# A fused two-expert feed-forward layer: direct block products in the first step, the second layer's tiles in one row, splits in two groups, another mix at the end

## The chip, the cores and the metric

The kernel runs on one core of a Trainium2 chip. The metric is device time in microseconds for one execution, from runs on the chip. Before the change the median of three runs is 2035.06 us (2034.77 to 2036.32).

## What is computed

For each of 8 batches, with x of 512 tokens by 512 features, a shared feed-forward network and one of five experts, chosen by the batch's label, are applied to the same x, and mixed by a gate that looks at token 0 only:

```python
ffn(x, wi0, wi1, wo) = (gelu(x @ wi0) * (x @ wi1)) @ wo          # 512 -> 2048 -> 512
share_out  = ffn(x, sWi0, sWi1, sWo)
expert_out = ffn(x, Wi0[label], Wi1[label], Wo[label])
gate_in = concatenate([expert_out[:, 0], share_out[:, 0]])
w = softmax(relu(gate_in @ g0) @ g1)
out = x + expert_out * w[0] + share_out * w[1]
```

All arrays are float32.

## The kernel before, in words

**Steps.** There are 128 steps: 8 batches, in each the shared network and then the expert, in each of those 8 steps of 256 hidden units. A step works on a 2 by 2 block scheme (two halves of the hidden units, two halves of the features, two halves of the tokens). Seven block products P1 to P7 of sums of blocks take the place of eight; the sums of weight blocks are made by VectorE (`weight_sums`, L493 to L515: one of 512 elements per partition, one of 1024 that makes two sums, one of 512), those of x by GpSimd once for each batch (`moving_sums`, L670).

**Splits.** TensorE multiplies in the type fp32r. Each operand is split in a high part, which ScalarE casts (`a_hi` L356, `x_hi` L366, `wo_hi`, `hid_hi` L391), and a low part, which VectorE makes by a subtraction (`lo`, L491). Each product of the reference is then three matmuls (low by high, high by low, high by high). The seven weight operands are split in groups of 3, 3 and 1, always for the step after the present one (`ahead(g)`). The high and low weights (`a_op`) have one buffer, the loaded weights (`a_src`) two, the split hidden units (`hs`) two.

**TensorE's order** is written out by hand (`step`, L281). A block product (`product`, L263) is 12 matmuls of 256 columns; one tile of the second layer (`second`, `down` L273) is 6 matmuls of 512 columns into `ps_out`. A step is P1, P5, tile 3, P6, P2, tile 0, P7, P3, tile 1, P4, tile 2. Tiles 0 to 2 use the hidden units of the step before, tile 3 those of two steps before. All engines execute their queue in the order of the program and wait on semaphores.

**ScalarE** copies partial products between PSUM banks (`p1_copied`, `v_copied`, `u_copied`, L426 to L449) and into `p5`, takes the three Gelus of a step (L398), and makes the high parts. After step 3 of a shared pass it takes the exponential of the gate (`exponentials`, L461).

**VectorE** (`step`, L533) makes, in this order: the weight sums for the next step, the low part of Wo, the low parts ahead, the product for block 11 (L554), the additions for blocks 22 and 12 (L558, L560), the product of 512 elements (L562), that for block 21 (L565), the remaining low parts ahead, and last the low part of this step's hidden units. Between two steps stands the gate's work (`one_pass`, L621): `gate_half` (L572, four dot products) after expert step 3; `gate_half` and the logits after shared step 1; `shift_logits` after shared step 2; `gate_weights` and `combine_shared` (2048 elements per partition) after shared step 3; `combine_expert` (L618) after shared step 4. The last six belong to the batch before, so the first batch's shared pass has none.

**SyncE** issues every DMA in its program order: Wo for the next step once the raw buffer is free, then the weights for the step after that, group by group.

**The start and the end.** In the first step the seven products are split one by one in the order P1, P5, P6, P2, P7, P3, P4. After the last step, the gate of the last batch is computed with nothing beside it. ScalarE and VectorE then scale tiles of the shared output, GpSimd adds x to two of them (L707), and VectorE adds the expert's tiles (L661), each of which is stored as it is ready.

Of the kernel before, what the change touches and what calls it, by code (L numbers as in the profile page):

```python
# [5 lines left out]
F32 = mybir.dt.float32  # L6
# [7 lines left out]
P = 128  # L14
# [17 lines left out]
ORDER = (P1, P5, P6, P2, P7, P3, P4)  # L32


GROUPS = [(0, 3), (3, 6), (6, 7)]
LAST_OF = (P6, P3, P4)
# [5 lines left out]
def splits(m, g):  # L42

    if m == 0:
        return GROUPS[g][1]
    return m * 3 + (PRODUCTS - 3 + g + 1)


def build(nc, x_cols, x_rows, labels, experts, shared, g0_rows, g1_rows, out):
# [10 lines left out]
    with ExitStack() as ctx:  # L60
# [14 lines left out]
        hs = [[sb(f"hid{s}{p}", [P, 2, TOK], F32R) for p in "hl"] for s in range(2)]  # L75
# [28 lines left out]
        ps_p5 = bank("ps_p5")  # L104
        ps_c11 = bank("ps_c11")
        ps_v = bank("ps_v")
# [3 lines left out]
        def halves(ps):  # L110
            return ps[:, :].rearrange("p (a t) -> p a t", a=2)
# [18 lines left out]
        wo_ready = sem("wo_ready")  # L130
        p_done = [sem(f"p_done{i}") for i in range(PRODUCTS)]
# [23 lines left out]
        last_scaled = sem("last_scaled")  # L155
        last_based_pool = sem("last_based_pool")
        last_based_dve = sem("last_based_dve")
        last_mixed = sem("last_mixed")

        block = ctx.enter_context(nc.Block())  # L160

# [13 lines left out]
        def _(sp):  # L175
# [23 lines left out]
            def first_loads():  # L199
                load_a(SHARED, None, 0, 0, 0, 0, first_a[P1])  # L200
                load_b(x_cols[0], 0, 0, first_b[P1])
                load_a(SHARED, None, 0, 0, 1, 0, first_a[P7])
                load_a(SHARED, None, 0, 0, 1, 1, first_a[P4])
                load_b(x_cols[0], 0, 1, first_b[P7])
                load_b(x_cols[0], 1, 1, first_b[P3])
                load_a(SHARED, None, 0, 0, 0, 1, first_a[P2])
                load_b(x_cols[0], 1, 0, first_b[P2])
                for i, j in A_PLACE:
                    load_a(SHARED, None, 1, 1, i, j, w_loaded[1])
                load_wo(SHARED, None, 0)  # L210
                sp.dma_start(labels_sb[:, :], labels).then_inc(labels_loaded, 16)

            def next_x(b):

                sp.wait_ge(x_ready, splits(b, 2))
                cols = x_cols[bass.ds(b + 1, 1)].rearrange("b p k t -> (b p) k t")
                for j, k in B_PLACE:
                    load_b(cols, j, k, x_loaded)

            def one_pass(b, net, n0, first, last):  # L220
# [5 lines left out]
                for c in range(STEPS):  # L226

                    ahead = c + 1
# [3 lines left out]

                    ahead = c + 2
                    if not (last and ahead >= STEPS):
                        of = net if ahead < STEPS else 1 - net
                        sp.wait_ge(a_ready, splits(n0 + c, 0))
                        load_a(of, label, ahead % STEPS, c % 2, 0, 0, w_loaded[c % 2])
                        sp.wait_ge(a_ready, splits(n0 + c, 1))
                        load_a(of, label, ahead % STEPS, c % 2, 0, 1, w_loaded[c % 2])
                        load_a(of, label, ahead % STEPS, c % 2, 1, 0, w_loaded[c % 2])  # L240
                        sp.wait_ge(a_ready, splits(n0 + c, 2))
                        load_a(of, label, ahead % STEPS, c % 2, 1, 1, w_loaded[c % 2])
# [19 lines left out]
        def _(pe):  # L262
            def product(i, ps, fresh):  # L263
                for a in (GATE, LIN):
                    for k in range(2):
                        for h, (ap, xp) in enumerate(PASSES):
                            mm = nc.tensor.matmul(ps[:, a * HALF:(a + 1) * HALF], a_op[ap][:, i, a, k, :],  # L267
                                                  x_op[xp][:, i, k, :],
                                                  start=(fresh and a == 0 and k == 0 and h == 0),
                                                  stop=(a == 1 and k == 1 and h == 2), skip_group_check=True)  # L270
                mm.then_inc(p_done[i], 1)

            def down(m, s, start, stop):  # L273
                for f in range(2):
                    for h, (hp, wp) in enumerate(PASSES):
                        mm = nc.tensor.matmul(ps_out[m][:, :], hs[s][hp][:, f, m * P:(m + 1) * P], wo[s][wp][:, f, :],  # L276
# [3 lines left out]

            def step(n, c, b, net, first, last):  # L281


                s = c % 2
                very_first = first and c == 0
                new_x = net == SHARED and c == 0

                def operands(i):
                    if very_first:
                        pe.wait_ge(a_ready, ORDER.index(i) + 1)  # L290
                        pe.wait_ge(x_ready, ORDER.index(i) + 1)
                    elif i in (P1, P2, P4):
                        g = (P1, P2, P4).index(i)
                        pe.wait_ge(a_ready, splits(n, g))
                        if new_x:
                            pe.wait_ge(x_ready, splits(b, g))

                def second(m):
                    before = 2 if m == MC - 1 else 1
                    if first and c < before:  # L300
                        return
                    of = (c - before) % STEPS
                    if m == 0:
                        pe.wait_ge(hid_ready, n)
                        pe.wait_ge(wo_ready, n)
# [5 lines left out]
                operands(P1)  # L311
                if not very_first:

                    pe.wait_ge(product_done, n * 3 - 2)
                product(P1, ps_c11, True)
                operands(P5)
                if not very_first:
                    pe.wait_ge(c12_done, n)
                product(P5, ps_p5, True)
                second(3)  # L320
                operands(P6)
                pe.wait_ge(p1_copied, n + 1)
                product(P6, ps_v, False)
                operands(P2)
                product(P2, ps_c11, False)
                second(0)
                operands(P7)
                pe.wait_ge(v_copied, n + 1)
                product(P7, ps_v, False)
                operands(P3)  # L330
                product(P3, ps_p5, False)
                second(1)
                operands(P4)
                pe.wait_ge(u_copied, n + 1)
                product(P4, ps_c21, False)
                second(2)

            def one_pass(b, net, n0, first, last):
                for c in range(STEPS):
                    step(n0 + c, c, b, net, first, last)  # L340

            pe.wait_ge(idle_ready, 1)

            for i in range(IDLE_MATMULS):
                nc.tensor.matmul((ps_v if i % 2 else ps_c21)[:, :], idle[:, 0:P], idle[:, :], start=True, stop=True)
            schedule(one_pass)

            down(3, 0, False, False)
            pe.wait_ge(hid_ready, N_STEPS)
            pe.wait_ge(wo_ready, N_STEPS)  # L350
            for m in range(MC):
                down(m, 1, False, True).then_inc(last_down_done, 1)

        @block.scalar
        def _(sc):
            def a_hi(m, s, g):  # L356


                sc.wait_ge(p_done[LAST_OF[g]], m)

                sc.wait_ge(sums_done, m * 3 + (2 if g == 0 else 3))
# [3 lines left out]
            def x_hi(b, g, n):  # L365

                sc.wait_ge(p_done[LAST_OF[g]], n + 1)
                sc.wait_ge(x_sums_done, b * 4 + (3 if g < 2 else 4))
# [3 lines left out]
            def first_hi(i):  # L372
                if i in (P5, P6, P7, P3):
                    sc.wait_ge(sums_done, {P5: 1, P6: 2, P7: 2, P3: 3}[i])
                else:
                    sc.wait_ge(first_a[i], 16)
                nc.scalar.copy(a_op[HI][:, i, :, :, :], a_src[0][:, i, :, :, :]).then_inc(a_hi_done, 1)
                if i in (P5, P6, P7, P4):
                    sc.wait_ge(x_sums_done, {P5: 1, P7: 2, P6: 3, P4: 4}[i])
                else:  # L380
# [3 lines left out]
            def wo_hi(n, s, free):  # L384
                sc.wait_ge(wo_loaded, n * 32 + 32)
                if free:
# [4 lines left out]
            def hid_hi(n, s, free):  # L391
                sc.wait_ge(product_done, n * 3 + 3)
                if free:
                    sc.wait_ge(down_done, n * MC - MC)
                nc.scalar.copy(hs[s][HI][:, :, :], act[:, LIN, :, :]).then_inc(hid_hi_done, 1)
# [3 lines left out]

            def step(n, c, b, net, first, last):  # L400
                s = c % 2
                very_first = first and c == 0
# [3 lines left out]
                free = not first or c > 1  # L406
# [3 lines left out]

                def ahead(g):
                    if not very_last:
                        a_hi(n + 1, 1 - s, g)
                    if new_x:
                        x_hi(b + 1, g, n)
# [5 lines left out]
                sc.wait_ge(p_done[P1], n + 1)  # L421
                if not very_first:

                    sc.wait_ge(c22_done, n)
                    sc.wait_ge(c12_done, n)
                nc.scalar.copy(ps_v[:, :], ps_c11[:, :]).then_inc(p1_copied, 1)  # L426
                if not first and c == 1:
                    copy_out(2)
                sc.wait_ge(p_done[P5], n + 1)
                nc.scalar.copy(p5[:, :, :], halves(ps_p5)).then_inc(p5_saved, 1)  # L430
                wo_hi(n, s, free)
                if not first and c == 1:
                    copy_out(3)
                sc.wait_ge(p_done[P6], n + 1)
                sc.wait_ge(p5_saved, n + 1)
                nc.scalar.copy(ps_p5[:, :], ps_v[:, :]).then_inc(v_copied, 1)
# [315 lines left out]
```

## Time and profile before

| | before |
|---|---|
| median of 3 runs | 2035.06 us |
| the profiled execution's own time | 2034.56 us |
| its span, first to last instruction | 2032.8 us |
| granted TensorE clock, mean | 0.995 |
| TensorE matmul busy | 2006.0 us (99%) |
| VectorE busy | 1631.2 us (80%) |
| ScalarE busy | 1221.1 us (60%) |
| GpSimd busy | 87.7 us (4%) |

Matmuls are pipelined and overlap, so busy time alone does not say how fast TensorE runs; the distance between the starts of two neighbours does. In the rows, PE is TensorE's matmul part, PEld its weight loads, DVE VectorE, ACT ScalarE, POOL GpSimd, SP SyncE. L12 is line 12 of the kernel. Times are microseconds unless marked ns, and start times count from the start of the span.

### The profile page before, as it was taken

The numbers are of one execution on the slowest core, as the hardware profiler recorded it, in microseconds if no ns is written. First come the engines' busy times: TensorE is split into PE (matmuls) and PEld (weight loads), VectorE is DVE, ScalarE is ACT, GpSimd is POOL, SyncE is SP. The second block draws the span as 40 slices with busy tenths as digits, with TensorE's granted clock in tenths as the row PEclk, the third lists the DMA queues.
The fourth block names the chain that finished last, engine by engine and source line by source line (L and its number), as shares of the span: only waits on it lengthen the run. The fifth ranks groups of instructions, "written<-read, shape, count | busy, mean of one in ns | idle before, by whom it ended". The sixth has DMA issues, their size and how long they took to land.

```text
span 2032.8 us, 34874 instructions
## 1 busy us (share of the span) xinstructions
PE 2006.0 (99%) x13834; PEld 1869.4 (92%) x13834; DVE 1631.2 (80%) x1917; ACT 1221.1 (60%) x1665; POOL 87.7 (4%) x62
## 2 busy tenths in 40 slices
PE   7999999999999999999999999999999999999997
PEld 6999999999999999999999999999999999999996
DVE  8778888787887878878788787887878878788785
ACT  6555566655666566655665656666566665665653
POOL 1001000010000100001000010000100010000000
PEclk8999999999999999999999999999999999999998
DMA  5333333433334332243333433344333433324330
GB/s 197 105 114 115 94 94 122 138 115 115 96 102 135 120 120 94 95 155 124 96 94 118 157 99 94 113 131 130 99 98 116 135 115 118 101 94 147 114 94 31
DMA packets 188020, 230.87 MB, mean 114 GB/s; under 512 B 13266, under 2 KB 152530, under 8 KB 185810
## 3 DMA queue, kind: packets, MB, share of 16 engines
q1 hardware_dynamic: 187858, 228.65, 35.3%
q8 instruction: 109, 1.79, 0.4%
q14 instruction: 53, 0.43, 0.1%
HBM read 220.21 MB, written 8.39 MB: 112 GB/s over the span
## 4 chain that ended last, share of the span: by engine, by line
PE 97%; DVE 1%; DMA 0%; ACT 0%; POOLq 0%; issue 0%; SPq 0%; POOL 0%; ACTq 0%
PE ps_out L276 35%; PE ps_c L267 27%; PE ps_p L267 18%; PE ps_v L267 18%; DVE al L491 0%; DMA a_src<-shared 0%; POOLq L60 0%; DVE xl L491 0%; DVE gate_prod L581 0%; ACT ah L363 0%; DVE a_src L515 0%; SPq L191 0%; SPq L182 0%; DVE hid1l L491 0%; DVE a_src L511 0%
## 5 line engine op out<-in xcount | busy, mean ns | idle before, releaser
L491 DVE TENSOR_TENSOR al<-a_src,ah 128x1536 fp32r<-128x1536 f32 (+1 forms) x388 | 532.6, 1398 | 63.0 <-ACT ah L363 60.1
L363 ACT CAST ah<-a_src 128x1536 fp32r<-128x1536 f32 x381 | 451.8, 1186 | 69.4 <-DVE a_src L511 69.4
L267 PE MATMUL ps_c<-xh,al 128*128 128x256 f32 x1536 | 433.6, 282 | 1.5 <-DVE xl L491 0.8
L267 PE MATMUL ps_c<-xh,ah 128*128 128x256 f32 x1536 | 434.6, 283 | 0.0
L267 PE MATMUL ps_c<-xl,ah 128*128 128x256 f32 x1536 | 434.6, 283 | 0.0
L267 PEld LDWEIGHTS ps_c<-xh,al 128*128 128x128 f32 x1536 | 293.9, 191 | 13.3 <-issue 1.4
L267 PEld LDWEIGHTS ps_c<-xl,ah 128*128 128x128 f32 x1536 | 293.9, 191 | 9.8
L267 PE MATMUL ps_p<-xh,al 128*128 128x256 f32 x1024 | 290.5, 284 | 6.4 <-DVE xl L491 6.4
L267 PEld LDWEIGHTS ps_c<-xh,ah 128*128 128x128 f32 x1536 | 293.9, 191 | 0.0
L267 PE MATMUL ps_v<-xh,al 128*128 128x256 f32 x1024 | 289.2, 282 | 2.9 <-ACT ps_v L426 2.9
L267 PE MATMUL ps_p<-xl,ah 128*128 128x256 f32 x1024 | 290.3, 284 | 0.0
L267 PE MATMUL ps_p<-xh,ah 128*128 128x256 f32 x1024 | 290.3, 284 | 0.0
L267 PE MATMUL ps_v<-xh,ah 128*128 128x256 f32 x1024 | 290.3, 284 | 0.0
L267 PE MATMUL ps_v<-xl,ah 128*128 128x256 f32 x1024 | 290.2, 283 | 0.0
L398 ACT ACTIVATE act<-act 128x512 f32<-128x512 f32 x128 | 80.9, 632 | 244.4 <-DVE act L560 244.4
L267 PEld LDWEIGHTS ps_v<-xh,al 128*128 128x128 f32 x1024 | 196.0, 191 | 14.5 <-DVE al L491 2.1
L267 PEld LDWEIGHTS ps_v<-xl,ah 128*128 128x128 f32 x1024 | 196.1, 191 | 9.8
L276 PE MATMUL ps_out<-wo1h,hid1l 128*128 128x512 f32 x512 | 203.3, 397 | 0.5 <-DVE hid1l L491 0.5
L267 PEld LDWEIGHTS ps_p<-xh,al 128*128 128x128 f32 x1024 | 197.1, 192 | 6.6 <-issue 6.6
L276 PE MATMUL ps_out<-wo0h,hid0l 128*128 128x512 f32 x512 | 202.5, 395 | 0.0
L276 PE MATMUL ps_out<-wo0l,hid0h 128*128 128x512 f32 x512 | 202.3, 395 | 0.0
L276 PE MATMUL ps_out<-wo1l,hid1h 128*128 128x512 f32 x512 | 202.3, 395 | 0.0
(75 smaller groups left out, 3598.9 us busy)
## 6 DMA issues: line engine op xcount, KB each, us to landing
a_src<-shared SPq DMA_DIRECT2D x256, 256.0 KB, 4.3
a_src<-experts SPq DMA_DIRECT2D x256, 256.0 KB, 4.2
raw_wo<-shared SPq DMA_DIRECT2D x128, 256.0 KB, 2.9
raw_wo<-experts SPq DMA_DIRECT2D x128, 256.0 KB, 2.8
x_src<-x_cols SPq DMA_DIRECT2D x32, 256.0 KB, 5.8
x_res<-x_rows SPq DMA_DIRECT2D x8, 1024.0 KB, 10.1
out<-s_out SPq DMA_DIRECT2D x7, 1024.0 KB, 8.4
g_sb<-g_rows SPq DMA_DIRECT2D x1, 2048.0 KB, 9.6
```

The lines of the kernel that those rows point to most:

```text
L267: mm = nc.tensor.matmul(ps[:, a * HALF:(a + 1) * HALF], a_op[ap][:, i, a, k, :], x_op[xp][:, i, k, :], start=(fresh and a == 0 and k == 0 ...
L276: mm = nc.tensor.matmul(ps_out[m][:, :], hs[s][hp][:, f, m * P:(m + 1) * P], wo[s][wp][:, f, :], start=(start and f == 0 and h == 0), stop ...
L363: nc.scalar.copy(a_op[HI][:, i:j, :, :, :], a_src[s][:, i:j, :, :, :]).then_inc(a_hi_done, 1)
L398: nc.scalar.activation(to, of, ACT.Gelu_apprx_tanh).then_inc(gelu_done, 1)
L491: nc.vector.tensor_tensor(to, of, hi.bitcast(F32), ALU.subtract).then_inc(done, 1)
```

## The change

**First step.** Step 0 takes eight products of the blocks as they are loaded, with no sums. VectorE makes the sums of x for the first batch. **Row of four.** In steps 1 to 127 the four tiles of the second layer stand in one row, after P2, all from the hidden units of the step before; in the very last step two stand there and two after P4. The split hidden units have one buffer. **Two groups.** The weight operands are split in groups of 4 and 3; the second group of a step's own weights is split in that step. The Gelu and the product of block 21, and the split of the hidden units, move to the head of the next step in ScalarE's and VectorE's queues. SyncE issues the weights before Wo. **End.** The last split of hidden units is in two parts, VectorE alone adds x and the scaled shared output, and GpSimd's and ScalarE's part in this goes.

The diff, cut to its core:

```diff
-GROUPS = [(0, 3), (3, 6), (6, 7)]
-LAST_OF = (P6, P3, P4)
+GROUPS = [(0, 4), (4, 7)]
+LAST_OF = (P2, P4)
...
-        hs = [[sb(f"hid{s}{p}", [P, 2, TOK], F32R) for p in "hl"] for s in range(2)]
+        hs = [sb(f"hid{p}", [P, 2, TOK], F32R) for p in "hl"]
...
@@ tensor @@
+            def first_step():
+                pe.wait_ge(a_ready, 1)
+                pe.wait_ge(x_ready, 1)
+                product(P1, P1, ps_c11, True)
+                pe.wait_ge(a_ready, 2)
+                pe.wait_ge(x_ready, 2)
+                product(P2, P2, ps_c11, False).then_inc(direct_done, 1)
...
+                product(P7, P7, ps_v, True)
+                product(P4, P3, ps_v, False).then_inc(direct_done, 1)
...
+                pe.wait_ge(a_ready, a_splits(n, 0))
...
+                pe.wait_ge(product_done, n * 3 - 2)
+                product(P1, P1, ps_c11, True).then_inc(p_done[P1], 1)
...
+                product(P5, P5, ps_p5, True).then_inc(p_done[P5], 1)
+                moving(P6)
+                pe.wait_ge(p1_copied, n)
+                product(P6, P6, ps_v, False).then_inc(p_done[P6], 1)
+                product(P2, P2, ps_c11, False).then_inc(p_done[P2], 1)
+                pe.wait_ge(hid_ready, n)
+                pe.wait_ge(wo_ready, n)
+                very_last = last and c == STEPS - 1
+                for m in range(2 if very_last else MC):
+                    second(m)
+                pe.wait_ge(a_ready, a_splits(n, 1))
...
+                product(P7, P7, ps_v, False).then_inc(p_done[P7], 1)
+                product(P3, P3, ps_p5, False).then_inc(p_done[P3], 1)
...
+                product(P4, P4, ps_c21, False).then_inc(p_done[P4], 1)
...
@@ scalar, step @@
+                c21_gelu()
+                sc.wait_ge(p_done[P1], n)
...
+                nc.scalar.copy(ps_v, ps_c11[:, :]).then_inc(p1_copied, 1)
+                hid_hi(n - 1, 0, TOK)
...
+                nc.scalar.copy(p5[:, :, :], halves(ps_p5)).then_inc(p5_saved, 1)
+                a_hi(n, s, 1)
...
+                nc.scalar.copy(ps_p5, ps_v).then_inc(v_copied, 1)
+                if not very_last:
+                    a_hi(n + 1, 1 - s, 0)
...
@@ scalar, end @@
-                nc.scalar.activation(s_out[:, m, :], s_out[:, m, :], ACT.Copy, scale=gate_w[:, SHARED:SHARED + 1]
-                                     ).then_inc(last_scaled, 1)
...
@@ vector, step @@
+                c21_product(n - 1)
+                if not very_last:
+                    weight_sums(n + 1, 1 - s, 0)
+                    weight_sums(n + 1, 1 - s, 1)
+                hid_lo(n - 1, 0, TOK)
...
+                    weight_sums(n + 1, 1 - s, 2)
+                a_lo(n, s, 1)
...
+                    a_lo(n + 1, 1 - s, 0)
...
+                dve.wait_ge(hid_ready, n)
+                c11_product(n)
+                wo_lo(n, s)
...
@@ vector, end @@
+            combine_shared(BATCH - 1)
+            dve.wait_ge(mixed, BATCH * 2 - 1)
             for m in range(MC):
-                if m < MC // 2:
-                    dve.wait_ge(last_based_dve, m + 1)
-                else:
-                    dve.wait_ge(last_based_pool, m + 1 - MC // 2)
                 dve.wait_ge(last_down_done, m + 1)
...
@@ gpsimd, end @@
-            pool.wait_ge(x_res_loaded, BATCH * 16)
-            for m in range(MC // 2, MC):
-                pool.wait_ge(last_scaled, m + 1 - MC // 2)
-                nc.gpsimd.tensor_tensor(s_out[:, m, :], x_res[:, m, :], s_out[:, m, :], ALU.add
-                                        ).then_inc(last_based_pool, 1)
```

The additions for blocks 22 and 12 and the product of 512 elements still end VectorE's step, and the gate's work still stands between two steps, at the same places.

## Rows read from the trace of the kernel before

**Rows 1.** The page's busy time of each engine, share of the span, instructions.
```profile
PE 2006.0 (99%) x13834; PEld 1869.4 (92%) x13834; DVE 1631.2 (80%) x1917; ACT 1221.1 (60%) x1665; POOL 87.7 (4%) x62
```
**Rows 2.** The chain that ended last, in order of time: start, length, what.
```profile
38.58 1.44 PE ps_p L267 x12
40.02 1.39 PE ps_out L276 x6
...
44.23 1.43 PE ps_c L267 x12
```
**Rows 3.** Timeline around the last step's end: start, length, engine, line, operation, tiles.
```profile
2006.69 0.69 DVE L560 TENSOR_TENSOR act<-ps_p,p 128x512 f32<-128x512 f32 x1
...
2007.47 0.63 ACT L398 ACTIVATE act<-act 128x512 f32<-128x512 f32 x1 [1.66 <-DVE act L560]
...
2008.14 0.69 DVE L562 TENSOR_TENSOR act<-act 128x512 f32<-128x512 f32 x1 [0.76 <-ACT act L398]
...
2009.19 0.28 PE L267 MATMUL ps_c<-xh,ah 128*128 128x256 f32 x1
...
2009.51 0.38 ACT L398 ACTIVATE act<-ps_c 128x256 f32<-128x256 f32 x1 [1.40 <-PE ps_c L267]
...
2009.93 0.42 DVE L565 TENSOR_TENSOR act<-act,ps_c 128x256 f32<-128x256 f32 x1 [1.09 <-ACT act L398]
...
2010.38 1.05 ACT L395 CAST hid1h<-act 128x1024 fp32r<-128x1024 f32 x1 [0.49 <-DVE act L565]
...
2011.47 1.23 DVE L491 TENSOR_TENSOR hid1l<-act,hid1h 128x1024 fp32r<-128x1024 f32 x1 [1.12 <-ACT hid1h L395]
...
2012.74 0.50 PE L276 MATMUL ps_out<-wo1h,hid1l 128*128 128x512 f32 x1 [0.53 <-DVE hid1l L491]
...
2014.24 0.39 PE L276 MATMUL ps_out<-wo1h,hid1l 128*128 128x512 f32 x1
...
2015.60 0.39 PE L276 MATMUL ps_out<-wo1h,hid1l 128*128 128x512 f32 x1
```
**Rows 4.** Timeline of VectorE where the gate's work stands between two steps.
```profile
203.04 0.68 DVE L581 CUSTOM_DVE_ANT_0 gate_prod<-g_sb,gate_row 128x512 f32<-128x512 f32 x1
...
205.85 0.69 DVE L506 TENSOR_TENSOR a_src<-a_src 128x512 f32<-128x512 f32 x1
...
296.79 0.75 DVE L581 CUSTOM_DVE_ANT_0 gate_prod<-g_sb,gate_row,gate_sum 128x512 f32<-128x512 f32 x1
...
300.34 0.69 DVE L506 TENSOR_TENSOR a_src<-a_src 128x512 f32<-128x512 f32 x1
301.07 1.23 DVE L511 TENSOR_TENSOR a_src<-a_src 128x1024 f32<-128x1024 f32 x1
...
327.99 0.16 DVE L603 RECIPROCAL gate_inv<-gate_den 128x1 f32<-128x1 f32 x1
...
330.71 0.69 DVE L506 TENSOR_TENSOR a_src<-a_src 128x512 f32<-128x512 f32 x1
```
**Rows 5.** Groups by line on VectorE: the expert's mixing, one each batch but the last.
```profile
L618 DVE SCALAR_TENSOR_TENSOR s_out<-x_src,gate_w,s_out 128x2048 f32<-128x2048 f32 x7 | 16.4, 2346 | 0.0
```
**Rows 6.** Timeline of ScalarE around one exponential of the gate.
```profile
325.76 1.28 ACT L463 ACT_TABLE_LOAD   x1
...
334.25 1.28 ACT L398 ACT_TABLE_LOAD   x1
```
**Rows 7.** Timeline of VectorE where GpSimd's sums of x begin.
```profile
171.84 1.78 DVE L506 TENSOR_TENSOR a_src<-a_src 128x512 f32<-128x512 f32 x1
```
**Rows 8.** Busy time of one early stretch by engine; third from last the granted clock.
```profile
14.30:20.00 5.70, 3.86 (x16) 3.60 (x17) 5.70 (x9) 5.70 (x11) 0.96 (x1) 0.50 0.00 0
```
**Rows 9.** Timeline of VectorE in the first step.
```profile
9.97 0.81 DVE L515 TENSOR_TENSOR a_src<-a_src 128x512 f32<-128x512 f32 x1 [0.85 <-DMA a_src<-shared]
```
**Rows 10.** Timeline of VectorE at the end.
```profile
2021.08 0.23 DVE L605 TENSOR_SCALAR gate_w<-gate_exp,gate_inv 128x2 f32<-128x2 f32 x1
...
2029.39 0.75 DVE L661 SCALAR_TENSOR_TENSOR s_out<-ps_out,gate_w,s_out 128x512 f32<-128x512 f32 x1 [0.47 <-POOL s_out L708]
```

More of the change, by code:

```diff
@@ L226, in one_pass @@
                 for c in range(STEPS):
+                    ahead = c + 2
+                    if not (last and ahead >= STEPS):
+                        of = net if ahead < STEPS else 1 - net
+                        sp.wait_ge(a_ready, a_splits(n0 + c, 0))
+                        load_a(of, label, ahead % STEPS, c % 2, 0, 0, w_loaded[c % 2])
+                        load_a(of, label, ahead % STEPS, c % 2, 0, 1, w_loaded[c % 2])
+                        sp.wait_ge(a_ready, a_splits(n0 + c, 1))
+                        load_a(of, label, ahead % STEPS, c % 2, 1, 0, w_loaded[c % 2])
+                        load_a(of, label, ahead % STEPS, c % 2, 1, 1, w_loaded[c % 2])
                     ahead = c + 1
@@ L262, in _, with product @@
         def _(pe):
-            def product(i, ps, fresh):
+            def product(i, j, ps, start):
                 for a in (GATE, LIN):
@@ L279, in down, with moving @@
                 return mm
-            def step(n, c, b, net, first, last):
[L284 to L296, printed above, removed]
-                def second(m):
[L299 to L305, printed above, removed]
+            def first_step():
[5 more added lines that the diff above has]
+                product(P2, P2, ps_c11, False).then_inc(direct_done, 1)
+                pe.wait_ge(x_ready, 3)
+                product(P1, P7, ps_p5, True)
+                pe.wait_ge(x_ready, 4)
+                product(P2, P3, ps_p5, False).then_inc(direct_done, 1)
+                pe.wait_ge(a_ready, 3)
+                product(P7, P1, ps_c21, True)
+                pe.wait_ge(a_ready, 4)
+                product(P4, P2, ps_c21, False).then_inc(direct_done, 1)
+                product(P7, P7, ps_v, True)
+                product(P4, P3, ps_v, False).then_inc(direct_done, 1)
+            def step(n, c, b, net, first, last):
+                def moving(i):
+                    if n == 1 and i in (P5, P6, P7, P4):
+                        pe.wait_ge(x_ready, {P5: 5, P6: 6, P4: 7, P7: 8}[i])
+                    if n > 1 and net == SHARED and c == 0 and i in (P1, P7):
+                        pe.wait_ge(x_ready, x_splits(b, 0 if i == P1 else 1))
+                def second(m):
+                    of = (c - 1) % STEPS
                     if of == 0 and not first:
@@ L323, in step @@
[L323 to L336, printed above, removed]
+                pe.wait_ge(a_ready, a_splits(n, 0))
@@ L338, in one_pass @@
+                moving(P4)
+                pe.wait_ge(u_copied, n)
+                product(P4, P4, ps_c21, False).then_inc(p_done[P4], 1)
+                if very_last:
+                    for m in range(2, MC):
+                        second(m)
             def one_pass(b, net, n0, first, last):
-                for c in range(STEPS):
+                for c in range(1 if first else 0, STEPS):
                     step(n0 + c, c, b, net, first, last)
@@ L397, in gelu, with c21_gelu, first_step @@
             def gelu(to, of):
                 nc.scalar.activation(to, of, ACT.Gelu_apprx_tanh).then_inc(gelu_done, 1)
+            def c21_gelu():
+                gelu(act[:, GATE, 1, 0:HALF], ps_c21[:, 0:HALF])
+            def first_step():
+                for i in (P1, P2):
+                    first_a_hi(i)
+                    first_x_hi(i)
+                for i in (P7, P3):
+                    first_x_hi(i)
+                for i in (P7, P4):
+                    first_a_hi(i)
+                a_hi(1, 1, 0)
+                for i, done in ((P5, 1), (P6, 2), (P4, 3)):
+                    sc.wait_ge(x_sums_done, done)
+                    first_x_hi(i)
+                gelu(act[:, GATE, 0, 0:HALF], ps_c11[:, 0:HALF])
+                wo_hi(0, 0)
+                sc.wait_ge(direct_done, 4)
+                sc.wait_ge(x_sums_done, 4)
+                nc.scalar.copy(x_op[HI][:, P7, :, :], x_src[:, P7, :, :]).then_inc(x_hi_done, 1)
+                gelu(act[:, GATE, :, HALF:TOK], ps_pv[:, :, 0:HALF])
@@ L431, in step @@
[L431 to L436, printed above, removed]
-                ahead(0)
-                sc.wait_ge(p_done[P2], n + 1)
+                if n > 1:
+                    sc.wait_ge(p_done[P4], n - 1)
+                c21_gelu()
+                sc.wait_ge(p_done[P1], n)
@@ L444, in step @@
-                    copy_out(0)
-                sc.wait_ge(p_done[P7], n + 1)
-                if not very_first:
-                    sc.wait_ge(product_done, n * 3)
-                nc.scalar.copy(ps_c21[:, :], ps_v[:, :]).then_inc(u_copied, 1)
-                sc.wait_ge(c22_done, n + 1)
-                sc.wait_ge(c12_done, n + 1)
-                gelu(act[:, GATE, :, HALF:TOK], act[:, GATE, :, HALF:TOK])
-                ahead(1)
-                if not first and c == 0:
-                    copy_out(1)
@@ L456, in step @@
-                sc.wait_ge(p_done[P4], n + 1)
-                gelu(act[:, GATE, 1, 0:HALF], ps_c21[:, 0:HALF])
-                ahead(2)
-                hid_hi(n, s, free)
+                        sc.wait_ge(x_ready, x_splits(b, 0))
+                    for m in range(MC):
+                        copy_out(m)
+                sc.wait_ge(p_done[P7], n)
+                sc.wait_ge(product_done, n * 3)
+                nc.scalar.copy(ps_c21[:, :], ps_v).then_inc(u_copied, 1)
+                sc.wait_ge(c22_done, n)
@@ L466, in one_pass @@
             def one_pass(b, net, n0, first, last):
-                for c in range(STEPS):
+                for c in range(1 if first else 0, STEPS):
                     step(n0 + c, c, b, net, first, last)
@@ new lines, in step @@
+            def step(n, c, b, net, first, last):
+                s = c % 2
+                very_last = last and c == STEPS - 1
+                c21_product(n - 1)
[3 more added lines that the diff above has]
+                hid_lo(n - 1, 0, TOK)
+                if n == 1:
+                    first_x_lo(P7, 8)
+                if not very_last:
+                    weight_sums(n + 1, 1 - s, 2)
+                a_lo(n, s, 1)
+                if n > 1 and net == SHARED and c == 0:
+                    x_lo(b, 1)
+                if not very_last:
+                    a_lo(n + 1, 1 - s, 0)
+                if net == EXPERT and not last and c == STEPS - 1:
+                    x_lo(b + 1, 0)
+                dve.wait_ge(hid_ready, n)
+                c11_product(n)
+                wo_lo(n, s)
+                dve.wait_ge(u_copied, n)
+                dve.wait_ge(p5_saved, n)
@@ L621, in one_pass @@
             def one_pass(b, net, n0, first, last):
-                for c in range(STEPS):
-                    step(n0 + c, c, b, net, first, last, (n0 + c + 2) // 2)
+                for c in range(1 if first else 0, STEPS):
+                    step(n0 + c, c, b, net, first, last)
                     if net == EXPERT and c == 3:
```

277 lines of the change are left out of this document (128 added, 149 removed).

## The prediction

> **What bounds the kernel now.** I read the page's busy time first: TensorE is busy for 2006.0 of 2032.8 us, no other engine for more than 80% [rows 1]. Busy matmuls overlap, so I then read the chain that ended last, in order of time. From about 44 us to 2009 us it consists of TensorE's own pieces, one directly behind the other: a product takes 1.44 us, a tile of the second layer 1.39 us [rows 2]. Seven products and four tiles make 7 × 1.44 + 4 × 1.39 = 15.64 us, a step's period to the rounding (15.61 without it). So in the middle only two things count: TensorE's own pace, and whether a wait of TensorE that is free today stops being free. The start and the end stand beside that.
>
> **The pace of the row of four.** Each six-matmul tile of the steady part takes 1.39 us, always behind a product [rows 2]. After the last step four tiles stand in a row: the second starts at 2014.24, the third at 2015.60, so a tile behind a tile takes 1.36 us [rows 3]. The row of four gains 3 × 0.03 = 0.09 us a step. A part is lost: a product behind a tile takes 1.43, one behind a product 1.44 [rows 2], and three such neighbours fewer cost 0.03. Net 0.06 us in each of 126 steps: **−7.6 us**. The Trainium skill (TensorE: Matmul & The Clock Gate, section "Wait — 56ns, not 53.3ns?") gives a warm matmul's start-to-start as N ÷ 2.4 GHz plus about 2.5 ns, whatever stands beside it, 216 ns for 512 columns. By that rule the order gains nothing and this term is zero. The rows show 232 and 227 ns per matmul (1.39 and 1.36 by six), and depend on the neighbour, so I take the rows.
>
> **Whether the waits stay free, ordinary step.** I lay the new queues beside TensorE's, T = 0 at the first matmul of P1. P2 ends and the row of four begins at T = 4 × 1.44 = 5.76; with 1.39 + 3 × 1.36 it ends at 11.23, P4 at 15.54. The row waits for the low part of the hidden units of the step before. Its chain, from the latencies in rows 3:
> - P3's last matmul is at −1.56. A reader starts 0.32 behind the last matmul (2009.19 to 2009.51), so the addition for block 12 is at −1.24. Its Gelu is 0.78 later (2006.69 to 2007.47), −0.46; the product of 512 elements 0.67 later, +0.21. VectorE is free again at about 0.81.
> - Block 21's Gelu is at +0.20, its product on VectorE at 0.81, because VectorE is busy. Behind it stand the first sum (1.15) and the double sum (1.88, since 0.73 passes between those two starts [rows 4]), then at 3.02 the hidden units' low part. ScalarE copies P1's partial result at 1.64, then makes the high part at about 2.15; the low part follows 1.09 later [rows 3], at 3.24. TensorE can go on 1.27 later (2011.47 to 2012.74), at 4.51.
>
> That leaves 1.25 us of slack. P6 waits for ScalarE's copy, done at 2.2, needed at 2.88: free. The step's second weight group (1536 elements; about 1.5 us high, 1.7 low) is ready near 7, needed at 11.23: free. The first group ahead is ready near 10.2, needed at 15.54: free. One split operation fewer (7 operands in two groups instead of three) saves VectorE under 0.1 us, hidden. SyncE's new order brings weights before Wo; Wo's split is now only at about 8, so both are covered by several microseconds, at zero; so is the single buffer of hidden units, whose readers end at 11.23 before the new split at about 17.7. The new PSUM layout costs nothing.
>
> **Where they do not stay free.** The gate's work stands between two steps on VectorE. Before, the hidden units were already split when it began; now block 21's product and the hidden units' low part queue behind it. With extra work X at 0.81 the low part starts at 3.02 + X, TensorE can go on at 4.29 + X, and waits X − 1.47 at the row of four, with nothing else that it may do.
> - Half of the gate after expert step 3: X = 205.85 − 203.04 = 2.81 [rows 4], a wait of 1.34, 8 times: 10.7 us.
> - Half of the gate and the logits after shared step 1: X = 300.34 − 296.79 = 3.55 [rows 4], 2.08, 7 times: 14.6 us.
> - Gate weights and shared mixing after shared step 3: 330.71 − 327.99 = 2.72 of work [rows 4]. It needs the exponential first. ScalarE is free at 0.1, loads a table (1.28), and has the exponential at about 1.7; before, this fell in time that nobody needed. Work from 1.74 to 4.46 makes X = 3.65, a wait of 2.18, 7 times: 15.3 us. A second table load of 1.28 us before the next Gelu exists today too [rows 6]; it now comes before the copy that P6 needs, so some 0.9 of the 2.18 shows at P6.
> - Expert mixing after shared step 4: 2.35 us [rows 5], 2.26 to the next start, 0.79, 7 times: 5.5 us.
> - Each row or product behind a wait starts slower: the tile from 2012.74 takes 1.50 instead of 1.39 [rows 3]; 36 waits by 0.1: 3.6 us.
>
> Together **+49.7 us**. The shift of the logits (0.3 us) fits in the slack. Part of the slack is taken in 7 steps by GpSimd's sums of x, beside which VectorE's 0.69 us operation took 1.78 [rows 7]: up to 1.1 each; it should be just covered, 0 taken, +7.7 as the upper end.
>
> **The start.** Before, P1 of step 2 starts at 44.1 [rows 2]; at the half clock (1.2 GHz) TensorE spent 14.3 to 20 us [rows 8], after some 6 us with nothing to do. Now loads land in the order they are used: the seventh landed by 9.97 before [rows 9], the same place holds the seventh now. Splits of 0.6 to 0.7 us each let the eight products run from 6.2 to 18.7 with gaps under 1 us. Step 1's sums, splits of four operands, sums of x on VectorE and a Gelu table load put its P1 at about 24.6 and its row at 31.3 at full clock, so step 2 at 41.1: a gain of 3.0. But TensorE stands idle for 6 us before P1, as it did when the clock fell, and I charge 1.6 for a few microseconds at half: **−1.4 us**, between −3 and +1.
>
> **The end.** Before, P4's end lies at 2009.31 and the last four tiles start at 2012.74. Now after P4 come two tiles (2.75), then, because of the single buffer, high and low parts of a quarter: 0.25 until readable, 0.42, 0.42 and 0.04 make 3.88 until the last four can start, instead of 3.43. But before P4 this step holds two tiles (2.75) instead of three (4.17). 0.45 − 1.42 makes −0.97, of which the neighbours of the pace paragraph give back some: **−0.9 us**. The gate's chain is unchanged up to its weights (done at 2021.3 [rows 10]). Before, GpSimd's part held the last mixing until 2029.39; now VectorE mixes 2048 elements (2.35 [rows 5]) and starts the fourth tile at 2021.34 + 2.39 + 3 × 0.67 = 2025.74: 3.65 earlier; some 0.15 comes back as four stores lie closer: **−3.5 us**.
>
> **Sum.** −7.6 + 49.7 − 1.4 − 0.9 − 3.5 = **+36.3 us**. The profiled execution took 2034.56 (the median is 0.5 above, no difference here), so 2070.9 us; the last digit of the latencies is worth 0.3 to 1 us over 29 places, and I say **2070 us**.
>
> **Rivals.**
> - *The hidden units are in time (faster).* Place: the row's wait after the gate's work. Were the slack over 2.2 us larger than I worked out (it decides at X − 1.47 > 0 for the largest X of 3.65), the 49.7 go and −13.4 is left: 2021 us. For it: in the trace before, TensorE waits for nothing in these steps. Against: there the split stood ahead of the gate's work. 0.09. Part of it, a slack some 0.5 to 1 us larger (12 to 25 us less): 2045 to 2058: 0.12.
> - *No gain in pace.* If the 1.36 of the end, where other engines rest, is not reached in mid-step, the lost 0.03 stays: +3.8 in place of −7.6, 2082 us. 0.08.
> - *The clock falls at the waits.* A gap of 0.5 us at 2012.3 left it at full; one of 6 us ended at half [rows 8]. The new gaps lie between. Were it half for 8 us after each of the 22 places with over 1.3 us (8 + 7 + 7), 22 × 4 = 88 more: 2158 us. 0.05.
> - *Nothing to measure:* slack larger by 0.8 us and the exponential free; 2031 to 2039. 0.04.
> - The forecast: 0.62, between 2056 (slack 0.5 larger) and 2083 (GpSimd's 7.7 and no pace gain).
>
> A measurement here can tell 0.2%, 4 us. Faster holds the first rival, 0.09; same 0.04; slower all else, 0.87. The range 2050 to 2084 leaves out the first of these, the clock, no change, and a little of the part case.
>
> **What would show it.** In the profile after: the chain with VectorE's hidden-unit low part (line of `lo`) in 29 places and ScalarE's copy in 7; tiles 2 to 4 of a row at 1.36; an ordinary period of 15.54; four waits per batch at the row, about 1.3, 2.1, 2.2 (with P6's part) and 0.8 us; no GpSimd piece at the end. Wrong: TensorE's waits for hidden units sum to under 25 us, or stretches of half clock after 50 us.

## The result and the profile after

| | before | after |
|---|---|---|
| median of the runs | 2035.05 us (4) | 2073.1 us (4: 2070.88 to 2073.45) |
| ratio, 95% interval | | 1.0183 (1.0166 to 1.0201) |
| profiled execution | 2034.56 us | 2070.88 us |
| its span | 2032.8 us | 2069.1 us |

The change costs 38 us by the medians, 36.3 us by the two profiled executions, on which the sum below is made. The profiled execution is the shortest of its four, 2.2 us under their median; so where an experiment below is set against the changed kernel, the medians show some 2 us more than the profiles. The forecast was 2070, between 2050 and 2084. The page of the kernel after, busy time and the chain that ended last by engine:

```profile
PE 2008.9 (97%) x13846; PEld 1874.3 (91%) x13846; DVE 1612.3 (78%) x1780; ACT 1180.3 (57%) x1524; POOL 88.0 (4%) x56
...
PE 86%; DVE 11%; ACT 2%; issue 1%; DMA 0%; SPq 0%; POOL 0%; DVEq 0%; ACTq 0%; POOLq 0%
```

Beside [rows 1] VectorE and ScalarE are less busy than before (GpSimd is as before, 88.0 beside 87.7 us), and yet VectorE now holds 11% of the chain. An engine can do less and come later. The view of waits, TensorE's alone (line, whom it waited for, us in total, times, longest):

```profile
PE ps_out L276 <- DVE hidl L519: 34.4, 30, 1.9
PE ps_pv L267 <- ACT ps_pv L459: 6.9, 7, 1.0
PE ps_c L267 <- DVE act L574: 5.1, 1, 5.1
```

The first line is the second layer's first tile, 29 times in mid-run and once at the end; the second is P6 behind ScalarE's copy, 7 times; the third is the start. The view counts from a matmul's modelled end; by the distances between starts, which are used from here on, each wait is some 0.15 us longer. One of the thirty, in the timeline (VectorE's rows and TensorE's):

```profile
200.34 0.69 DVE L651 CUSTOM_DVE_ANT_0 gate_prod<-g_sb,gate_row 128x512 f32<-128x512 f32 x1
200.96 0.08 DVE L651 DVE_READ_ACCUMULATOR2_ANT gate_sum<- 128x1 f32 x1
200.96 0.41 DVE L579 TENSOR_TENSOR act<-act,ps_c 128x256 f32<-128x256 f32 x1
201.29 0.68 DVE L532 TENSOR_TENSOR a_src<-a_src 128x512 f32<-128x512 f32 x1
202.01 1.23 DVE L536 TENSOR_TENSOR a_src<-a_src 128x1024 f32<-128x1024 f32 x1
...
202.97 0.28 PE L267 MATMUL ps_c<-xh,ah 128*128 128x256 f32 x1
203.16 1.22 DVE L519 TENSOR_TENSOR hidl<-act,hidh 128x1024 fp32r<-128x1024 f32 x1
...
204.43 0.50 PE L276 MATMUL ps_out<-wo1h,hidl 128*128 128x512 f32 x1 [1.18 <-DVE hidl L519]
```

The last dot product of the gate, then block 21's product, two sums, the hidden units' low part, and 1.27 us after its start TensorE's tile: the queue of the prediction, piece by piece. P2's last matmul starts at 202.97; without the wait the tile would start 0.12 later, so 1.34 us are lost.

And the pace, in the chain in order of time, an ordinary step after [rows 2 show one before]:

```profile
46.41 1.44 PE ps_c L267 x12
47.85 5.47 PE ps_out L276 x24
53.32 2.87 PE ps_pv L267 x24
```

Four tiles take 5.47 us, not 4 × 1.39 = 5.56, and the two products behind them 2.87. The start-to-start distances of all matmuls give the whole account:

| part | before | after | difference |
|---|---|---|---|
| start of the span to P5 of step 2 | 45.50 | 43.37 | −2.13 |
| P5 of step 2 to P5 of step 127 | 1951.03 | 1993.88 | +42.85 |
| from there to TensorE's last matmul | 21.57 | 20.71 | −0.86 |
| from there to the end of the span | 14.69 | 11.15 | −3.54 |
| sum | 2032.8 | 2069.1 | +36.3 |

The second line holds 45.9 us of waits (below), 29 + 7 slow restarts of 0.11 and 0.10 (3.9 us) and one stretch at half clock (about 1.6, below), together 51.4. From this the pace goes off, 125 × 0.06 = 7.5 us (the ordinary period is 15.54 us, before 15.60), and 1.0 us more, because in the kernel before seven steps, the first of each new batch, were 0.15 longer than the others, and now are not.

### The profile page after: what moved, and what is told of

Read it like the earlier page. It is cut to its first block, busy times and chain, and to the rows that moved or that the text cites. A ratio compares the mean times of both kernels' runs of the same rounds, so it can differ in the third digit from the quotient of the medians.

```text
span 2069.1 us, 34457 instructions
## 1 busy us (share of the span) xinstructions
PE 2008.9 (97%) x13846; PEld 1874.3 (91%) x13846; DVE 1612.3 (78%) x1780; ACT 1180.3 (57%) x1524; POOL 88.0 (4%) x56
## 4 chain that ended last, share of the span: by engine, by line
PE 86%; DVE 11%; ACT 2%; issue 1%; DMA 0%; SPq 0%; POOL 0%; DVEq 0%; ACTq 0%; POOLq 0%
PE ps_out L276 34%; PE ps_pv L267 31%; PE ps_c L267 21%; DVE gate_prod L651 2%; DVE a_src L536 2%; DVE hidl L519 2%; DVE act L637 1%; ACT act L411 1%; DVE s_out L683 1%; DVE a_src L532 1%; DVE s_out L688 1%; DVE act L579 0%; ACT L492 0%; DMA a_src<-shared 0%; DVE act L639 0%
## 5 line engine op out<-in xcount | busy, mean ns | idle before, releaser
L519 DVE TENSOR_TENSOR al<-a_src,ah 128x1536 fp32r<-128x1536 f32 (+2 forms) x258 | 524.8, 2035 | 103.0 <-ACT ah L377 94.4
L267 PE MATMUL ps_pv<-xh,al 128*128 128x256 f32 x2048 | 580.0, 283 | 6.9 <-ACT ps_pv L459 6.9
L267 PE MATMUL ps_pv<-xl,ah 128*128 128x256 f32 x2048 | 579.9, 283 | 0.0
L267 PE MATMUL ps_pv<-xh,ah 128*128 128x256 f32 x2048 | 579.9, 283 | 0.0
L377 ACT CAST ah<-a_src 128x2048 fp32r<-128x2048 f32 x254 | 430.7, 1696 | 43.2 <-PE ps_c L267 38.8
L267 PEld LDWEIGHTS ps_pv<-xh,al 128*128 128x128 f32 x2048 | 393.1, 192 | 13.3 <-ACT ps_pv L459 8.3
L267 PEld LDWEIGHTS ps_pv<-xl,ah 128*128 128x128 f32 x2048 | 393.0, 192 | 5.0
L267 PEld LDWEIGHTS ps_pv<-xh,ah 128*128 128x128 f32 x2048 | 393.0, 192 | 0.0
L276 PE MATMUL ps_out<-wo1h,hidl 128*128 128x512 f32 x512 | 203.1, 397 | 30.0 <-DVE hidl L519 30.0
L276 PE MATMUL ps_out<-wo0h,hidl 128*128 128x512 f32 x512 | 200.8, 392 | 4.4 <-DVE hidl L519 4.4
```

What stands on the lines that cost most here:

```text
L276: mm = nc.tensor.matmul(ps_out[m][:, :], hs[hp][:, f, m * P:(m + 1) * P], wo[s][wp][:, f, :], start=(start and f == 0 and h == 0), stop=(s ...
L377: nc.scalar.copy(a_op[HI][:, i:j, :, :, :], a_src[s][:, i:j, :, :, :]).then_inc(a_hi_done, 1)
L519: nc.vector.tensor_tensor(to, of, hi.bitcast(F32), ALU.subtract).then_inc(done, 1)
```

## The experiments

All times are medians beside runs of the kernel before on the same chip (2034.9 to 2035.3 us).

**1. The gate's work behind the hidden units.**

```diff
+            def gate_between(b, net, first, c):
+                if net == EXPERT and c == 4:
+                    gate_half(b, 0, SHARED)
...
                 hid_lo(n - 1, 0, TOK)
+                gate_between(b, net, first, c)
...
                     step(n0 + c, c, b, net, first, last)
-                    if net == EXPERT and c == 3:
-                        gate_half(b, 0, SHARED)
```

> The changed kernel, with one edit: on VectorE the gate's work that stood between two steps stands one place later, behind the low part of the hidden units in the next step; ScalarE's exponential stays where it is. Theory (queue order): the row of four waits only because block 21's product and the hidden units' low part queue behind the gate's work. The waits at the row, 8 x 1.34, 7 x 2.08, 7 x 1.03 and 7 x 0.79 us in the profile after, go with their slow restarts (29 x 0.11), together 36 to 42 us; the 1.14 us at P6 after the exponential stays, 7 times. Time about 2031 us. Rival (VectorE's load): the gate's work is too much for VectorE in those steps wherever it stands; then the waits reappear at other products and the time stays near 2073 us.

Measured: 2029.11 us, ratio to the kernel before 0.997 (0.9958 to 0.9982). 44.0 us are gone against the changed kernel, 2 more than the upper end of what was expected; by the profiled spans 41.9 (2069.1 to 2027.2). The waits at rows in mid-run are gone, the seven at P6 stand as they were:

```profile
PE ps_pv L267 <- ACT ps_pv L459: 6.9, 7, 1.0
PE ps_c L267 <- DVE act L574: 5.1, 1, 5.1
```

Not one operation of VectorE was taken out, so its load is not the cause; its order is. Why P6 waits is in ScalarE's timeline of this kernel:

```profile
322.11 1.28 ACT L492 ACT_TABLE_LOAD   x1
323.41 0.20 ACT L492 ACTIVATE gate_exp<-logit_diff 128x2 f32<-128x2 f32 x1
...
323.72 1.28 ACT L411 ACT_TABLE_LOAD   x1
325.02 0.38 ACT L411 ACTIVATE act<-ps_c 128x256 f32<-128x256 f32 x1
325.30 0.59 ACT L459 COPY ps_pv<-ps_c 128x512 f32<-128x512 f32 x1
```

Two table loads and block 21's Gelu now stand ahead of the copy that P6 needs. Before, the second load stood behind that copy, and behind the next group's high part [rows 6].

**2. The exponential too.** It goes behind the high part of Wo in the next step, gate weights and mixings one step later.

```diff
                 wo_hi(n, s)
+                if c == 4 and net == SHARED and not first:
+                    exponentials(b - 1)
```

> As the kernel with the gate's work behind the hidden units' low part, and also ScalarE's exponential moved from the step's end into the next step, behind the high part of Wo, with gate weights and both mixings one step later. Queue order: the seven waits at P6 (1.14 + 0.10 us each, 8.7 us) go too, about 2023 us, that is 12 us under the kernel before. This is the whole price of the gate's place, about 50 us against the changed kernel. Rival (load): as for the first, no gain. Second rival: ScalarE's two table loads, now ahead of the copy that P4 needs, make P4 wait; then about 2023 + 7 x 1 us.

Measured: 2019.77 us, ratio 0.9923 (0.9908 to 0.9938). TensorE waits for nothing between the start and the last tile row. All of TensorE's waits in this profile are these, the first three in the start and the fourth in the last tile row:

```profile
PE ps_c L267 <- DVE act L574: 5.1, 1, 5.1
PE ps_c L267 <- DVE xl L519: 2.6, 2, 2.2
PE ps_out L355 <- DVE idle L711: 1.2, 1, 1.2
PE ps_out L276 <- DVE hidl L519: 1.1, 1, 1.1
```

The kernel takes 53.3 us less than the changed kernel where about 50 were forecast; by the profiled spans it is 50.5 (2069.1 to 2018.6). The stretch from P5 of step 2 to P5 of step 127 is 51.4 shorter, which is the waits, the restarts and the half clock of the table above (51.4); the start of this execution was 0.8 longer. Neither rival shows. This kernel is faster than both, by 0.8% than the kernel before.

**3. The law of the slack.**

```diff
+                hid_lo(n - 1, 0, TOK)
                 if not very_last:
                     weight_sums(n + 1, 1 - s, 0)
                     weight_sums(n + 1, 1 - s, 1)
-                hid_lo(n - 1, 0, TOK)
```

> The changed kernel, with one edit: on VectorE the hidden units' low part stands ahead of the first two sums of weights instead of behind them; the gate's work is not moved. Queue order gives a law: the wait is X minus the slack. The low part can now start 0.04 us after ScalarE's high part, at 2.36 + X instead of 3.02 + X, so each wait shrinks by 0.66 us: 0.68, 1.42, 1.52 (with P6's part) and 0.13 us. Sum 8 x 0.68 + 7 x (1.42 + 1.52 + 0.13) = 27 us instead of 46: 19 us less, 2054 us. Rival (VectorE's load): the same work in another order, no change, 2073 us. Rival (the wait comes from ScalarE's high part, not from VectorE): the low part could not start earlier, no change.

Measured: 2055.99 us, 17.1 less than the changed kernel, 14.7 by the profiled spans. The waits at the row go from 37.9 to 18.9 us, as the law asks (19 less): 1.42 is the longest, 0.13 the shortest. A wait that I had not seen takes some back: seven times P5 waits 0.58 us (4.1 in all) for the addition of block 12, which ends later.

```profile
PE ps_out L276 <- DVE hidl L519: 15.6, 23, 1.3
PE ps_pv L267 <- ACT ps_pv L459: 6.9, 7, 1.0
...
PE ps_pv L267 <- DVE act L637: 2.9, 7, 0.4
```

**4. The other half of the cause.** In the kernel before, the gate's work is moved ahead of the hidden units' low part.

```diff
                 ahead(2)
+                if net == EXPERT and c == 3:
+                    gate_half(b, 0, SHARED)
...
                 dve.wait_ge(hid_hi_done, n + 1)
```

> The kernel before, with the gate's work on VectorE moved ahead of the hidden units' low part, the place that it has in the changed kernel, all else as before. Law of the slack: there the low part starts 1.85 us after P1 begins, TensorE can have it 1.27 us later, at 3.1, and tile 0 stands at 4 x 1.44 + 1.39 = 7.15 us: slack 4.0 us, over the largest X (3.55; the exponential is off the path there, since it follows the high part). So no wait, 2035 us. Rival (work of the gate ahead of the hidden units always costs): 29 waits of about 2 us, 2090 us. If the first holds, the earlier place of tile 0 and the later split are the other half of the cause, beside the gate's place.

Measured: 2035.3 us, ratio 1.0 (0.9991 to 1.0009). The same place in the queue costs nothing there; TensorE's one wait for hidden units in this profile is that of the last row, which the kernel before has too:

```profile
PE ps_out L276 <- DVE hid1l L491: 0.5, 1, 0.5
```

It takes both: the gate's work ahead of the hidden units, and a slack of 1.25 in place of 4.0 us. That the row of four behind P2 and the later split have made the slack small is worked out from the start times; no run moved one of these two alone.

**5. The pace, first try.** Three tiles in a row in the kernel before:

```diff
                 product(P5, ps_p5, True)
-                second(3)
...
+                second(3)
                 second(0)
+                second(1)
```

> The kernel before, with one edit on TensorE: tile 3 of the second layer stands behind P2, directly ahead of tiles 0 and 1, and tile 2 stays behind P4. Nothing else is changed. Theory (a tile behind a tile is faster): two of four tiles stand behind a tile and take 1.36 instead of 1.39 us, and two products fewer stand behind a tile: 0.06 - 0.015 = 0.045 us in each of about 127 steps, 5 to 6 us less, about 2029.5 us. Rival (the start-to-start of the Trainium skill, TensorE: Matmul & The Clock Gate, that doesn't ask for the neighbour): no change, 2035 us.

Measured: 2098.27 us, ratio 1.031 (1.0296 to 1.0324). I missed this one: 5 to 6 us less were expected, 63 more came. Tile 3 had been the cover of P6. TensorE's largest group of waits:

```profile
PE ps_v L267 <- ACT ps_v L426: 42.7, 30, 3.0
```

and ScalarE's timeline of the same kernel (the last line is TensorE's). The high part of Wo waits until tile 3, the last to read its buffer, is done, 3.73 us here (before 0.85):

```profile
239.79 1.05 ACT L389 CAST wo0h<-raw_wo 128x1024 fp32r<-128x1024 f32 x1 [3.73 <-PE ps_out L276]
240.74 0.58 ACT L436 COPY ps_p<-ps_v 128x512 f32<-128x512 f32 x1
241.26 1.48 ACT L363 CAST ah<-a_src 128x1536 fp32r<-128x1536 f32 x1
...
268.90 0.58 ACT L426 COPY ps_v<-ps_c 128x512 f32<-128x512 f32 x1
...
269.53 0.39 PE L267 MATMUL ps_v<-xh,al 128*128 128x256 f32 x1 [2.99 <-ACT ps_v L426]
```

Everything behind it on ScalarE and VectorE moves back, up to the next copy for P6. The last two lines show the worst case, where ScalarE also casts the new batch's x. By the start times P6 waits in 66 of the 125 steps of mid-run, 51.2 us in all, with 6.3 of slow restarts. Some 8.6 us more are half clock: at five of the seven longest waits, 3.14 us each, the granted clock fell to half.

It shows what a moved tile can cost when its waits are not laid out first, which I had not done here. On the pace the forecast was right all the same: the 59 steps in which P6 does not wait take 15.56 us each, before 15.60, and 0.045 less was expected.

**6. The pace, second try.** The changed kernel with the row of four broken in two.

```diff
-                for m in range(2 if very_last else MC):
+                for m in range(2):
                     second(m)
...
                 product(P7, P7, ps_v, False).then_inc(p_done[P7], 1)
+                if not very_last:
+                    for m in range(2, MC):
+                        second(m)
```

> The changed kernel, with the row of four broken in two: tiles 0 and 1 behind P2, tiles 2 and 3 behind P7. Theory of pace: one tile more stands behind a product (1.39 instead of 1.36 us) and one product more behind a tile (0.01 less), so the ordinary period grows from 15.54 to 15.56 us, 2.6 us over the run, 2075.7 us, with the waits at the first tile as they are. Rival (neighbours don't matter): 15.54 stays.

Measured: 2075.1 us, 2.0 over the changed kernel; the two intervals overlap (this one 1.018 to 1.0212), so the median alone decides nothing. The median distance from P5 to P5 is 15.56 us in this profile, 15.54 in the changed kernel and in both with the gate moved. The chain in order of time:

```profile
63.77 2.75 PE ps_out L276 x12
66.52 1.43 PE ps_pv L267 x12
67.95 2.75 PE ps_out L276 x12
70.70 1.43 PE ps_pv L267 x12
```

Two pairs take 5.50 us, the row of four 5.47, four single tiles 5.56, and each product behind a tile 1.43. With the 15.56 of experiment 5 these are three orders of the same matmuls, each with the period that its neighbours give. Why a neighbour matters stays open.

**7. The start.** The changed kernel with 22 idle matmuls in the 5.3 us gap ahead of step 1.

```diff
             first_step()
+            for i in range(22):
+                nc.tensor.matmul(ps_out[0][:, :], idle[:, 0:P], idle[:, :], start=True, stop=True)
             schedule(one_pass)
```

> The changed kernel, with 22 idle matmuls (zeros, 512 columns, into a bank that the next use overwrites) between the eight products of the first step and step 1, in the 5.3 us in which TensorE waits. Theory (the idle stretch brings the half clock): the clock stays at full, step 1's row begins about 1.2 us earlier (at about 31.0 us instead of 32.15), because at full clock P5 waits for VectorE's product. Rival: the half clock there has another cause; it falls as before, and the idle matmuls, slower then, end after 24.3 us and push step 1 back by up to 4 us. Neither can be told by the median; the profile tells.

Measured: 2072.5 us, no difference by the median. The same stretch by engine (third from last the granted clock), the changed kernel:

```profile
22.06:28.89 6.83, 4.59 (x21) 4.62 (x22) 5.15 (x8) 5.38 (x8) 0.00 (x0) 0.50 0.27 96
```

and with the gap filled:

```profile
22.06:28.89 6.83, 5.58 (x38) 4.24 (x37) 5.20 (x9) 5.92 (x10) 0.00 (x0) 1.00 0.25 77
```

The clock stays at its upper level (2.4 GHz), and step 1's row begins at 31.19 instead of 32.15, 0.96 earlier (1.2 expected); P5 of step 2 starts at 42.41 instead of 43.37. The span does not show it, because this execution had two short stretches at half clock later on where the other had one.

**8. The end alone, in the kernel before.** ScalarE's and GpSimd's part goes.

```diff
+            combine_shared(BATCH - 1)
+            dve.wait_ge(mixed, BATCH * 2 - 1)
             for m in range(MC):
-                if m < MC // 2:
-                    dve.wait_ge(last_based_dve, m + 1)
-                else:
-                    dve.wait_ge(last_based_pool, m + 1 - MC // 2)
```

> The kernel before, with the change's end alone: VectorE mixes the shared output and x in one operation and then the four tiles; ScalarE's and GpSimd's part in this is taken out. Expected from the chain at the end: GpSimd's part goes, the distance from TensorE's last matmul to the span's end falls from 14.7 to 11.2 us as in the changed kernel, 3.5 us less, 2031.8 us. Rival (the stores set the end: four stores now lie closer together and queue): less than 2 us.

Measured: 2031.5 us, ratio 0.9981 (0.9972 to 0.999), 3.7 us less. VectorE's last pieces in its timeline:

```profile
2022.58 2.35 DVE L609 SCALAR_TENSOR_TENSOR s_out<-s_out,gate_w,x_res 128x2048 f32<-128x2048 f32 x1
2024.97 2.73 DVE L650 SCALAR_TENSOR_TENSOR s_out<-ps_out,gate_w,s_out 128x512 f32<-128x512 f32 x4
```

From TensorE's last matmul to the span's end are 11.16 us, as in the changed kernel (11.15), instead of 14.69. The stores' rival does not show.

**9. Together: gate, exponential and filled gap.** The edits of 1, 2 and 7.

> The changed kernel with the gate's work behind the hidden units' low part, the exponential moved with it, and the 22 idle matmuls in the gap of the start. Both effects stand apart in time, so they add: 2019.8 less about 1.2 to 1.8 us, 2018.3 us, about 17 us (0.8%) under the kernel before. Rival: a step whose slack is nearly used up brings back a wait; then no better than 2019.8 us.

Measured: 2018.73 us, ratio 0.992 (0.9907 to 0.9934), 16.1 us under the kernel before and 54 under the changed one. Beside the kernel of experiment 2 (0.9923) the two intervals overlap, so the times do not show the idle matmuls' own 1 us. The profiles do: from the first matmul of step 1 to P5 of step 2 it takes 17.94 us with the gap filled (experiments 7 and 9), and 18.8 to 19.1 in the five profiles of this start without it.

## Why the prediction was right

Point by point, by its own terms:

- *Pace of the row*: −7.6 forecast. The period went from 15.60 to 15.54, 0.06 in 125 or 126 steps, −7.5. Against the whole of the middle of the kernel of experiment 2 (1942.50 us, no wait in it) the kernel before took 8.53 more; 1.0 of that lies outside its ordinary period, in the seven first steps of a batch, which the forecast did not count.
- *Waits*: 1.34, 2.08, 2.18 and 0.79 forecast for the four places, 46.1 us in the sum before restarts. Measured 1.34, 2.08, 2.17 (1.14 at P6 and 1.03 at the row) and 0.79, together 45.9. Restarts 0.11 and 0.10, forecast 0.1. The split of the third between P6 and the row was off (0.9 at P6 forecast), its sum not.
- *GpSimd's sums of x*: taken at 0, held at most 7.7 open; no wait appeared.
- *Start*: −1.4 forecast, −2.13 in this profile. The kernels of experiments 1 and 2, whose start is the same program, give 43.6 and 44.2 for P5 of step 2, those of 3 and 6, in which only step 1 has another order, 43.8 and 43.7, against 45.5, 46.6 and 45.8 in three profiles of the old start: −1.3 to −3.2. That TensorE would work at half clock after its idle stretch was right (from 22.06 to 28.89 us). Its price was taken too high: 1.6 charged, about 1 gone when the gap was filled. The forecast's times at full clock, 31.3 for the row and 41.1 for step 2, are met by that run with 31.19 and 40.97. (The 44.1 before is the start of P1's first matmul, 44.07; the chain in [rows 2], which goes by modelled ends, shows 44.23.)
- *End*: −0.9 forecast, −0.86 measured; −3.5 forecast, −3.54 measured, and shown by experiment 8.
- *Sum*: 36.3 forecast, 36.3 measured. This closeness is partly luck: the start gained 0.7 more than forecast and the middle 1.0 that was not counted, against 1.6 of half clock that the forecast did not have in its main case. One bound was added up wrong: the forecast's upper end of 2083, "GpSimd's 7.7 and no pace gain", is 2086 by these two terms and 2090 with the lost 0.03 a step of the rival; neither case came.

The rivals. "The hidden units are in time" fell by experiments 1 and 3: the waits are X − 1.47 us as laid out, to a few hundredths, and they go when the gate's work goes from the place. "No gain in pace" fell by the period of 15.54 in the profile after, and by experiments 5 and 6. "The clock falls at the waits" is true in a small part: in the profile after, once in 22 places the clock went to half (1.2 GHz), behind a wait of 2.09 us, and for 3.4 us only, at a cost of about 1.6 us, not 4. At longer waits it comes more often, in five of the seven of 3.14 us in experiment 5. The other runs of the changed kernel took 2 to 2.6 us more than the profiled one; more such stretches would explain it, and their mean granted clock is 0.995 where the profiled one's is 0.996, but no trace of those runs exists, so this is argued only.

What let the prediction hold was that it did not stop at the question whether VectorE has time in a step (it has: 12 of 15.5 us) but laid both queues beside TensorE's with the latencies of [rows 3].

## What to carry to other kernels

When an operation is moved to the head of the next round in a queue, look at what stands between the rounds: rare work there (gates, mixing, a table load) was free as long as it came last, and now stands ahead of something urgent. Work out the slack of the tightest wait once, from the pieces' start times, and hold every rare piece against it; a busy share of 78% says nothing on this. And a tile that is moved uncovers whatever waited behind it: experiment 5 lost 63 us for 6.

## What the runs showed that I had not expected

- In the first tile behind a product the starts of 512-column matmuls lie 231 ns apart on average, from the second tile on 227 ns (the profile after); a 256-column matmul needs 120 ns, but the first behind a tile only 113. The order of the same matmuls is worth 0.4% of this kernel.
- The clock can fall after a gap of only 2.1 us, though rarely: in three profiles (after, experiments 6 and 7) at 1, 1 and 2 of the 7 places with this wait, never at the shorter ones; behind the 3.14 us of experiment 5 at 5 of 7. One such stretch, in the timeline's busy time by engine of the kernel after:

```profile
1066.00:1070.00 4.00, 3.52 (x8) 2.78 (x9) 3.98 (x4) 3.89 (x5) 0.00 (x0) 0.57 0.04 9
```

The stretches behind these waits lasted 3.4 us, one in experiment 5 6.8 us; those of the start lasted 6.8 us (after) and 10.2 us (before).
